# A transformer layer on one core: the stretch between the projections and the first attention head, with a store let run on, loads reordered and set-up work moved

## The reference, cut to what matters

```python
nq = _rms(x @ w_cq, g_qnorm)                      # queries through a latent of 96
q = concat([q_nope, rope(q_rope)])                # 16 heads, 32 + 64 wide
k1, v1 = ...                                      # LATENT branch: from ckv, causal
scores = (x @ w_imp)[..., 0]
_, idx = top_k(scores, KEEP); idx = sort(idx)     # KEEP = 64 tokens
sel = take_along_axis(x, idx)                     # SELECT branch
ks = (sel @ w_selk) ; vs = (sel @ w_selv)
ks = concatenate([ks[..., :NOPE], _rope(ks[..., NOPE:], cos, sin)])
kw, vw = ...                                      # WINDOW branch: from x, causal
a1 = _attn(q, k1, v1, causal=True)
a2 = _attn(q, ks, vs, causal=False)
a3 = _attn(q, kw, vw, causal=True)
out = (g[:, 0] * a1 + g[:, 1] * a2 + g[:, 2] * a3) ... @ w_proj
```

## Time and profile before

| what | us |
|---|---|
| runs, median (lowest to highest) | 2511.4 (2511.3 to 2516.3), 3 runs |
| the profiled execution, its own time | 2516.76 |
| its span in the trace | 2515.0 |
| PE busy in the span | 2213.3 (88%) |
| DVE, ACT, POOL busy | 1869.1 (74%), 1722.3 (68%), 1655.6 (66%) |
| project ends, select begins | 300.2, 310.8 |
| SP begins select's last two issues, attend begins | 377.3, 380.9 |

### The profile page before, as it was taken

One profiled execution on the slowest core, in us unless ns is written; L12 is line 12 of the kernel. 1 busy time (PEld: TensorE's weight loads), 2 busy tenths in 40 slices (PEclk: granted clock), 3 DMA queues, 4 the chain that ended last, 5 costly groups with the idle time before them and its releaser, 6 DMA issues. The chain is left out here.

```text
span 2515.0 us, 37523 instructions
## 1 busy us (share of the span) xinstructions
PE 2213.3 (88%) x11426; PEld 1863.4 (74%) x11426; DVE 1869.1 (74%) x3842; ACT 1722.3 (68%) x3574; POOL 1655.6 (66%) x1425
## 2 busy tenths in 40 slices
PE   0077678999999999999999999999999998368997
PEld 0054446888888888888888888888888886368997
DVE  2656466878888887888888788888888884356775
ACT  2433405787888878788887878888888887115775
POOL 4145506878787887878787787877777777013554
PEclk9986568999999999999999999999999999657999
DMA  9856637244444423444442434232133110624774
GB/s 380 360 186 200 237 98 213 64 93 101 95 131 98 114 77 97 95 97 134 99 114 77 98 95 96 83 68 58 31 74 71 31 18 19 153 92 136 226 211 122
DMA packets 191126, 304.34 MB, mean 121 GB/s; under 512 B 97420, under 2 KB 121484, under 8 KB 177996
## 3 DMA queue, kind: packets, MB, share of 16 engines
q1 hardware_dynamic: 181211, 289.58, 41.2%
q0 software_dynamic: 9712, 12.36, 2.4%
HBM read 206.01 MB, written 97.30 MB: 121 GB/s over the span
## 5 line engine op out<-in xcount | busy, mean ns | idle before, releaser
L1433 POOL TENSOR_TENSOR p_lo<-prob,p_hi 128x512 fp32r<-128x512 f32 (+3 forms) x1040 | 1210.6, 1180 | 372.4 <-ACT p_hi L1515 344.5
L1513 ACT ACTIVATE prob<-ps_s 128x512 f32<-128x512 f32 (+4 forms) x1344 | 727.3, 541 | 307.1 <-DVE ps_s L1759 184.0
L1515 ACT ACTIVATE p_hi<-ps_s 128x512 fp32r<-128x512 f32 (+3 forms) x1344 | 726.3, 540 | 1.6
L1651 DVE TENSOR_REDUCE max_part<-ps_x 128x1 f32<-128x512 f32 x744 | 504.4, 685 | 54.6 <-PE ps_x L1562 45.8
L1433 DVE TENSOR_TENSOR p_lo<-prob,p_hi 128x512 fp32r<-128x512 f32 (+2 forms) x240 | 214.0, 892 | 66.3 <-ACT p_hi L1515 64.3
L1649 DVE CUSTOM_DVE_ANT_0 ps_x<-ps_x,before 128x128 f32<-128x128 f32 x496 | 243.1, 492 | 25.4 <-PE ps_x L1562 19.0
L1617 PE MATMUL ps_o<-p_hi,v_lat 128*128 128x512 f32 (+3 forms) x640 | 239.4, 374 | 0.6 <-POOL p_lo L1433 0.6
L1617 PE MATMUL ps_o<-p_hi,v_win 128*128 128x512 f32 (+3 forms) x640 | 236.6, 370 | 0.0
L1619 PE MATMUL ps_o<-p_lo,v_win 128*128 128x512 f32 (+3 forms) x640 | 235.1, 367 | 0.0
L1619 PE MATMUL ps_o<-p_lo,v_lat 128*128 128x512 f32 (+3 forms) x640 | 234.6, 367 | 0.0
L1759 DVE TENSOR_TENSOR ps_s<-ps_s,mask_kq 128x128 f32<-128x128 f32 x512 | 151.7, 299 | 54.0 <-PE ps_s L1534 47.4
(11 more groups left out here) (441 smaller groups left out, 5718.9 us busy)
## 6 DMA issues: line engine op xcount, KB each, us to landing
raw<-in_experts_w_dram SPq DMA_DIRECT2D x23, 1536.0 KB
wbuf<-in_tok_weight_dram SPq DMA_DIRECT2D x16, 2000.0 KB, 16.9
head_first<-kw_scratch SPq DMA_DIRECT2D x72, 256.0 KB, 5.0
kw_scratch<-st_hi SPq DMA_DIRECT2D x48, 256.0 KB, 2.3
kw_scratch<-st_lo SPq DMA_DIRECT2D x48, 256.0 KB, 3.0
q_scratch<-st_hi SPq DMA_DIRECT2D x48, 256.0 KB, 4.6
q_scratch<-st_lo SPq DMA_DIRECT2D x48, 256.0 KB, 5.2
head_first<-q_scratch SPq DMA_DIRECT2D x48, 256.0 KB, 5.9
```

What stands on the lines that cost most here:

```text
L1433: ns.tensor_tensor(upper if low else p_lo[:, i % LSLOTS, c:CH], prob[low:P, i % NPROB, c:CH], upper.bitcast(F32), ALU.subtract).then_inc(s ...
L1513: nc.scalar.activation(prob[low:P, i % NPROB, c:CH], ps_s[i % 3][low:P, c:CH], ACT.Exp, scale=SCALE).then_inc(s["p_full"], 1)
L1515: nc.scalar.activation(p_hi[:, i % SLOTS, c:CH], ps_s[i % 3][:, c:CH], ACT.Exp, scale=SCALE).then_inc(s["p_up"], 1)
L1651: ins = nc.vector.tensor_reduce(mpart[:, q, c:c + 1], bank[:, 0:w], axis=AX.X, op=ALU.max)
```

## The change

It has four parts.

1. `g.scratch` and two semaphores `v_stored` now live through `select`. `project` no longer waits for the values' stores, and the last one (the second half of the latent branch) is issued in `select`, behind the small tables; `select` waits for both at its end. To make room, the tables and split weights that only `project` needs are freed with it.
2. `select`'s loads come in another order: queries' and window keys' high parts, then `w_selk`, `w_selv`, the tables, the values' store, then the low parts.
3. `hot` is made in 2 instructions of 8 token tiles each in place of 16, from `slots + 1` and `(position + 1) * flag`; the keys' scaling goes from DVE to ACT, the rotation and the split of the selected values from DVE to POOL; 28 row-maximum units instead of 14 stand ahead of PE's wait for the rotated keys (`beside`).
4. In `attend`, the first head's `split_up` (ACT) and `split_low` (DVE) stand at unit 3, and the gate tiles and constants (`begin`) at unit 5 of head 0, in place of ahead of unit 0.

```diff
@@ -433,13 +433,9 @@
             for t in TASKS[-2:]:
                 for o in products(t):
                     store(o)
-            if TASKS[-1][0] == "v":
-                store_values(LATENT, 1)
             sp.wait_ge(s["ust"], 16 * NJ)
             sp.wait_ge(s["tst"], 32 * NJ)
             sp.wait_ge(s["lst"], 32 * NJ)
-            for n in range(2):
-                sp.wait_ge(s[f"vst{n}"], 32)
             for n in range(NO):
                 sp.wait_ge(s[f"st{n}"], 32 * len(range(n, len(MADE), NO)))
         maxima = [(t, c) for t in range(NT) for c in range(t // 4 + 1)]
-        early, middle = 0, 14
+        early, middle, beside = 0, 14, 28
...
-            sp.dma_start(wk[:], a["w_selk"].rearrange("(k p) n -> p k n", p=P)).then_inc(s["w"], 16)
-            sp.dma_start(wv[:], a["w_selv"].rearrange("(k p) n -> p k n", p=P)).then_inc(s["w"], 16)
             for n, (half, dram, sem) in enumerate(((q_hi, g.q_dram[0], "q"), (kw_hi, g.kw_dram[0], "kw"), (q_lo, g.q_dram[1], "low"), (kw_lo, g.kw_dram[1], "low"))):
                 for r in range(3):
                     row = (0, NOPE, NOPE + HALF)[r]
                     sp.dma_start(half[row:row + NOPE, :].bitcast(F32), dram[0, r, 0:NOPE, :]).then_inc(s[sem], 16)
                 if n == 1:
+                    sp.dma_start(wk[:], a["w_selk"].rearrange("(k p) n -> p k n", p=P)).then_inc(s["w"], 16)
+                    sp.dma_start(wv[:], a["w_selv"].rearrange("(k p) n -> p k n", p=P)).then_inc(s["w"], 16)
                     sp.dma_start(ck[:], a["cos_tok"]).then_inc(s["t"], 16)
                     sp.dma_start(sk[:], a["sin_tok"]).then_inc(s["t"], 16)
+                    sp.dma_start(g.v_dram[0, :, :, 8 * DV:16 * DV].rearrange("h p n -> p h n"),
+                                 g.scratch[:, 1, :].rearrange("p (h n) -> p h n", h=H)).then_inc(g.v_stored[1], 16)
             sp.wait_ge(s["khi"], 4)
             sp.wait_ge(s["c1"], 4)
             sp.dma_start(g.ks_dram[:, 0:QA, :].rearrange("h r k -> r h k"), khi[:].bitcast(F32)).then_inc(s["st"], 16)
                              nm_t[r * NT:(r + 1) * NT, :].bitcast(F32)).then_inc(s["rows"], 16)
+            for n in range(2):
+                sp.wait_ge(g.v_stored[n], 32)
...
+            r = Count(pool, s["rot"])
+            pool.wait_ge(s["ks_read"], 3)
+            pool.wait_ge(s["t"], 32)
+            x1, x2 = ktm[:, :, NOPE:NOPE + HALF], ktm[:, :, NOPE + HALF:DQK]
+            cb = ck[:].unsqueeze(1).to_broadcast([KEEP, H, HALF])
+            sbc = sk[:].unsqueeze(1).to_broadcast([KEEP, H, HALF])
+            r.add(nc.gpsimd.tensor_tensor(kt1[:], x1, cb, ALU.mult))
+            r.add(nc.gpsimd.tensor_tensor(kt2[:], x2, sbc, ALU.mult))
+            r.add(nc.gpsimd.tensor_tensor(kt3[:], x1, sbc, ALU.mult))
+            r.add(nc.gpsimd.tensor_tensor(kt4[:], x2, cb, ALU.mult))
+            r.add(nc.gpsimd.tensor_copy(krt[:, :, 0:NOPE], ktm[:, :, 0:NOPE]))
+            r.wait()
+            r.add(nc.gpsimd.tensor_tensor(krt[:, :, NOPE:NOPE + HALF], kt1[:], kt2[:], ALU.subtract))
+            r.add(nc.gpsimd.tensor_tensor(krt[:, :, NOPE + HALF:DQK], kt3[:], kt4[:], ALU.add))
+            r.wait()
+            pool.sem_inc(s["rope"], 1)
+            pool.wait_ge(s["vone"], 2)
+            r.add(nc.gpsimd.tensor_tensor(g.v_one[:, :, 2 * DV:3 * DV], vs[:], g.v_one[:, :, DV:2 * DV].bitcast(F32), ALU.subtract))
+            r.wait()
...
             for t in range(NT):
-                pe.wait_ge(s["hot"], t + 1)
+                pe.wait_ge(s["hot"], 2 * t // NT + 1)
...
                 done = max_products(done, early + (n + 1) * (middle - early) // 4)
+            done = max_products(done, beside)
             pe.wait_ge(s["rope"], 1)
...
+            act.wait_ge(s["selr"], 1)
+            for n in range(3):
+                act.wait_ge(s["ks"], n + 1)
+                nc.scalar.activation(ktm[:].rearrange("p h d -> p (h d)")[:, n * CH:(n + 1) * CH], bank[3 + n][0:KEEP, :], ACT.Copy,
+                                     scale=sel_rstd[:, 0:1]).then_inc(s["ks_read"], 1)
             act.wait_ge(s["ks"], 4)
-            act.wait_ge(s["selr"], 1)
...
+            v.add(nc.vector.tensor_scalar(slots1[:], g.slots[:], 1.0, None, ALU.add))
             dve.wait_ge(s["pos"], 1)
-            v.add(nc.vector.tensor_copy(pos[:], bank[0][:, 0:NT]))
+            v.add(nc.vector.scalar_tensor_tensor(pos[:], bank[0][:, 0:NT], 1.0, flag[:], ALU.add, ALU.mult))
             v.wait()
-
-            for t in range(NT):
-                nc.vector.tensor_scalar(hot[:, t, :], g.slots[:], pos[:, t:t + 1], flag[:, t:t + 1], ALU.is_equal, ALU.mult).then_inc(s["hot"], 1)
+            for n in range(2):
+                c = slice(n * NT // 2, (n + 1) * NT // 2)
+                nc.vector.tensor_tensor(hot[:, c, :], slots1[:].unsqueeze(1).to_broadcast([P, NT // 2, KEEP]),
+                                        pos[:, c].unsqueeze(2).to_broadcast([P, NT // 2, KEEP]), ALU.is_equal).then_inc(s["hot"], 1)
...
-            for n in range(4):
-                if n < 3:
-                    dve.wait_ge(s["ks"], n + 1)
-                    nc.vector.tensor_scalar(ktm[:].rearrange("p h d -> p (h d)")[:, n * CH:(n + 1) * CH], bank[3 + n][0:KEEP, :], sel_rstd[:, 0:1], None,
-                                            ALU.mult).then_inc(s["ks_read"], 1)
-                done = maxima_of(done, early + (n + 1) * (middle - early) // 4)
...
-            v.add(nc.vector.tensor_tensor(kt1[:], x1, cb, ALU.mult))
-            v.add(nc.vector.tensor_tensor(kt2[:], x2, sbc, ALU.mult))
...
-            v.add(nc.vector.tensor_copy(krt[:, :, 0:NOPE], ktm[:, :, 0:NOPE]))
...
-            v.add(nc.vector.tensor_tensor(krt[:, :, NOPE:NOPE + HALF], kt1[:], kt2[:], ALU.subtract))
-            v.add(nc.vector.tensor_tensor(krt[:, :, NOPE + HALF:DQK], kt3[:], kt4[:], ALU.add))
-            v.wait()
-            dve.sem_inc(s["rope"], 1)
+            done = maxima_of(done, beside)
             half = (done + len(maxima)) // 2
...
-            dve.wait_ge(s["vone"], 2)
-            v.add(nc.vector.tensor_tensor(g.v_one[:, :, 2 * DV:3 * DV], vs[:], g.v_one[:, :, DV:2 * DV].bitcast(F32), ALU.subtract))
...
-            split_up(0, WINDOW)
             for h in range(H):
                 for i in range(NU):
+                    if h == 0 and i == 3:
+                        split_up(0, WINDOW)
...
-            for b in range(NB):
-                r = ORDER.index(b)
-                nc.vector.tensor_copy(gates[:, r, :], g.gates[:, GATE[b]:GATE[b] + 1].to_broadcast([P, NT])).then_inc(s["gset"], 1)
-            for half, b in ((k1_hi, LATENT), (kw_hi[1], WINDOW)):
-                nc.vector.tensor_copy(half[DQK:QA, :], g.onehot[DQK:QA, b:b + 1].to_broadcast([NB, T])).then_inc(s["ones"], 1)
-            dve.wait_ge(s["set"], 1)
+            def begin():
+                for half, b in ((k1_hi, LATENT), (kw_hi[1], WINDOW)):
+                    nc.vector.tensor_copy(half[DQK:QA, :], g.onehot[DQK:QA, b:b + 1].to_broadcast([NB, T])).then_inc(s["ones"], 1)
+                for b in range(NB):
+                    r = ORDER.index(b)
+                    nc.vector.tensor_copy(gates[:, r, :], g.gates[:, GATE[b]:GATE[b] + 1].to_broadcast([P, NT])).then_inc(s["gset"], 1)
+                dve.wait_ge(s["set"], 1)
             held = [()]
-            split_low(0)
...
+                    if h == 0 and i == 3:
+                        split_low(0)
+                    if h == 0 and i == 5:
+                        begin()
...
+                g.scratch = tile("scratch", [P, 2, NT * C])
+                g.v_stored = [front.enter_context(nc.semaphore(f"v_stored{n}")) for n in range(2)]
                 with ExitStack() as small:
-                    g.scratch = small.enter_context(nc.sbuf_tensor("scratch", [P, 2, NT * C], F32, side="right"))
+                    tile = lambda n, s, d=F32: small.enter_context(nc.sbuf_tensor(n, s, d))
...
```

More of the change, by code:

```diff
@@ L362, in project @@
               "ls", "lrt", "lat", "lhi", "llo", "v", "x", "x_act", "x_dve", "less", "rank", "turn", "full_act", "full_dve", "full_pool",
-              "up", "low", "st0", "st1", "st2", "ust", "tst", "lst", "vst0", "vst1", "ranks")}
+              "up", "low", "st0", "st1", "st2", "ust", "tst", "lst", "ranks")}
         block = ctx.enter_context(nc.Block())
@@ L410, in store_values @@
                 sp.dma_start(g.v_dram[1 if b == WINDOW else 0, :, :, half * 8 * DV:(half + 1) * 8 * DV].rearrange("h p n -> p h n"),
-                             values[:, half].rearrange("p h t d -> p h (t d)")).then_inc(s[f"vst{half}"], 16)
+                             values[:, half].rearrange("p h t d -> p h (t d)")).then_inc(g.v_stored[half], 16)
             row_trip(0)
@@ L603, in _ @@
                     if i == LATENT and j % 8 == 0:
-                        act.wait_ge(s[f"vst{half}"], 16)
+                        act.wait_ge(g.v_stored[half], 16)
```

(40 more changed lines are left out.)

## The result

| | before | after |
|---|---|---|
| median of the runs | 2511.4 us | 2501.46 us (2497.63 to 2503.02, 5 runs) |
| ratio, with its 95% interval | | 0.9953 [0.9938, 0.9967] |
| profiled execution, its span | 2516.76, 2515.0 | 2502.49, 2500.8 |

The kernel is faster by 0.47%, 11.8 us of 2511.4 by the ratio, which compares the runs round by round; the two medians alone differ by 9.9. 2495.8 was forecast, 15.6 less than before, with a range of 2487.5 to 2504: the measured median lies in it, 5.7 above the forecast. In us the ratio's interval is 8.3 to 15.6. The gain lies where it was expected, but is smaller.

A forecast was written before the change was run, and what follows sets the result against it. PE, busy 88% of the span, was taken to bound the kernel, so gains come only where it starves. -9.2 + 0.7 - 7.1 + 0 = -15.6 us from 2511.4 gives 2495.8 us, range 2487.5 to 2504.

The forecast's parts named there:

- Border: From project to select: without SP's wait for the values' stores, select starts 9.2 us earlier, at 301.6 (bounds 8 and 9.2).
- First product: In select: weights behind six loads land late, so their first product starts S + 16.0, 0.7 us later (S: select's start).
- the values' rest costs 1.4 us: At select's start: the first values' half still occupies the queue until S + 1.4, ahead of the six loads and weights.
- PE's readiness: Before the first weight product: shorter `hot`, gather and scales leave PE ready at S + 13.5, 1.8 us earlier than before.
- Second half: From first weight product to select's last issue: work taken off DVE's chain saves 7.1 us (bounds 4 and 9.5).
- Three `ks_tok` of 0.74: In select after the first weight product: three key copies leave DVE for ACT, counted as 1.3 us saved.
- Rotation, wait and low part: In select's later stretch: 4.2 us for rotation, about 0.9 of the transposes' wait, 0.7 for the selected values' low part.
- The clock rival: At select's weight products: weights land at S + 19, four groups may run at half clock; 8.1 us more, 2503.9; chance 0.15.
- Rotation on GpSimd: In select: 1.35 us an instruction, chain of 9.1, hidden beside the maxima with 5.6 us of slack, so costs nothing.
- if that cover were gone, all 9.1 would show: In select: without maxima beside it, the whole 9.1 us of the GpSimd chain would lengthen the kernel.
- Attend, 0: At attend's start: the sine table's load still holds PE before `prep`, so 0 gained (bounds 3.4 gained, 3 lost).

The follow-up runs named there:

- Experiment 1: Changed kernel with both values' stores issued and waited for in project again: attend's start 379.21 us against 368.61.
- experiment 4: Changed kernel with rotation and low part back on DVE behind 14 maxima: first weight product to select's last issue 52.75 us, 5.55 more.
- experiment 6: Changed kernel with attend's set-up back in one piece ahead of unit 0: `prep` 16.67 us behind attend's start against 16.52.
- experiment 7: Changed kernel with the inputs of `prep` loaded before the keys: `prep` 10.30 us behind attend's start against 16.52.
- experiment 8: Changed kernel with the inputs of `prep` loaded before the keys and attend's set-up in one piece: `prep` 13.22 us behind attend's start.
- experiment 12: The changed kernel measured once more, nothing edited: 2503.49 us, ratio to the kernel before 0.9956.
- Experiment 3: Changed kernel with weights loaded ahead of the six loads and `hot` in 16 instructions again: first weight product 15.30 us behind select's start.
- experiment 5: Changed kernel with 14 maxima instead of 28 ahead of the transposes, rotation still on GpSimd: second half 50.57 us, 3.4 longer.
- the joined kernel: Changed kernel with weights loaded first, `prep` inputs loaded before the keys, and slots counted from one without `slots_one`: 2492.29 us, ratio to before 0.9913.

## Why the prediction was off by 5.7 us

- **Border, 9.2 us: right.** 9.16 measured by S, 9.4 counted from `ranks`, which leaves out the shift of what lies ahead; the 1.4 for the border itself came out as 1.40. Experiment 1 puts the wait back.
- **First product, 0.7 later: right.** 0.73 measured, released by the weights as forecast. The bytes went through as counted, and the lag to landing was 2.0 for the 2.1 assumed, which was the middle of 1 to 3.4 and no reading: that it hit so closely is luck. That the values' rest costs 1.4 us was wrong: in experiment 1 the empty queue lost as much by its own start. PE's readiness was off too, without effect: 2.4 + 7.1 + 3.6 is 13.1, not 13.5, and it was S + 14.1, since `slots_one` took 1.9 us ahead of `hot`.
- **Second half, 7.1 us: wrong, it was 4.0.** This is the step that failed, at its lower bound of 4, and by two terms. "Three `ks_tok` of 0.74, of which I count 1.3": worth 0, since that stretch was held by PE, for which DVE waited before as well (experiment 4). And one that I had only as a rival: one more group of products on the slow clock, 3.53 us for 1.93, so 1.6. Rotation, wait and low part gave 5.55 of the 5.8 forecast. 5.6 - 1.6 = 4.0. The other kernels bear the 1.6 out: in the eleven with the rotation on GpSimd behind 28 maxima, the second half took 44.8 to 45.9 us in the five where the second group ran in 1.93, and 47.2 to 47.4 in the six where it did not. And in the changed kernel it is chance whether it comes: its own select was profiled five times (the changed kernel, experiments 6, 7, 8 and 12), slow in three and in 1.93 in two. (The term's upper bound adds to 9.7, not 9.5: 2.2 + 4.2 + 2.6 + 0.7.)
- **The clock rival: half right, and not closed.** As written, with the weights at S + 19 and all four groups slow, it did not come. It gave a pause of PE as the reason for a late rise of the clock, and I put it at 0.15. Of the 14 profiled kernels the second group of products ran slow (3.46 to 3.68 us) in seven of the nine in which PE had paused for the weights (1.65 to 2.79 us), and in one of the five in which it had not. Experiment 3 is that one: no pause, 3.52 us. Experiments 7 and 8 paused and had 1.93. So the rise falls one group earlier or later; a pause is neither needed for the late one nor enough. That the late rise is more frequent behind a pause is the count of 14 executions, too few to show it. By the Trainium skill (TensorE: Matmul & The Clock Gate, section HAM oscillation) a pause for a transfer throttles PE again; no row here shows that, since the clock was 0.50 before the pause too. Its size was as priced, 1.6 us a group (1.7 forecast), but it befell one of the three later groups, not all three.
- **Rotation on GpSimd: right.** 1.26 us each where I took 1.35, a slack of 6.6 for 5.6. What failed is "if that cover were gone, all 9.1 would show": with it gone 3.4 us showed (experiment 5), for the rest of the rotation still lay beside the first 14 maxima. The Trainium skill's advice against the move (GPSIMD Engine Reference, section 4.1) holds for the instruction, 1.26 against 0.67 us, and not for the kernel.
- **Attend, 0: right within 0.4**, and its reason is shown by experiments 6 to 8.
- **The rest of the 5.7 us.** The front gave 11.9 of the forecast's 15.6 (12.1 counted from `ranks`), so some 3.6 are accounted for, and by the ratio's 11.8 that is the whole miss. The remaining 2 are the difference between the ratio's gain and that of the two medians, 9.9. The two profiled spans differ by 14.2; 2.3 of it lie behind `prep`, where nothing was changed. From `prep` to the load of `w_proj` at mix's start the runs with that stretch unchanged took 1750 to 1754 us, but one, and from there to the end 355 to 367: that is where the runs' spread of 5 us and more comes from. So a difference of two single spans proves nothing about the front; the marks do.

## What to carry to other kernels

Cut the trace at marks that the change cannot pass, and compare from mark to mark: a term of 1.5 us shows there that drowns in the times of whole runs. Work moved off a chain saves only what that chain alone was waiting for, so ask of each moved piece what else holds that stretch (here PE held the stretch of the copies, and a transfer that of attend's set-up). When an earlier start only lengthens the next wait for a transfer, the order of the issues is the thing to change: two lines moved gave 6 to 8 us here, where the set-up spread over units gave nothing without them.

## What the runs showed of the hardware

- **DVE and GpSimd hold each other up over SBUF.** `slots_one`, 128x64, took 1.90 us beside GpSimd's cast of 1.89, and ended with it. Without it `hot` was held up. DVE's row of the joined kernel, then rows of the one that holds GpSimd back:

```profile
303.26 2.25 DVE L951 TENSOR_TENSOR hot<-slots,pos 128x512 fp32r<-128x512 f32 x2
```

```profile
303.27 1.29 DVE L952 TENSOR_TENSOR hot<-slots,pos 128x512 fp32r<-128x512 f32 x2
...
304.67 1.95 DVE L958 TENSOR_SCALAR gates<-gate_tmp 128x3 f32<-128x3 f32 x1
...
304.70 1.89 POOL L818 CAST ks_hi_all<-onehot 3x2048 fp32r<-3x2048 f32 x1 [2.28 <-DVE hot L952]
```

 With GpSimd held back `hot` takes 1.29, and the instruction that then meets the cast, three elements wide, takes 1.95 (0.33 in the changed kernel). It goes the other way too: in attend GpSimd's `p_lo` took 2.32 us beside DVE's casts of 1.22 (378.67), and 1.27 at 376.33. The Trainium skill (SBUF — State Buffer, section Who interferes with whom) says that the two share a port that one holds at a time; the rows agree.
- **An issue behind a large store can take long.** SP's row of the changed kernel, then of experiment 1, whose select has no values' store ahead of these three loads:

```profile
308.30 10.51 SPq L782 DMA_DIRECT2D head_first<-q_scratch  x3
```

```profile
317.88 1.51 SPq L786 DMA_DIRECT2D head_first<-q_scratch  x3
```

 In the twelve kernels with the store right ahead the three issues took 10.2 to 10.8 us, in the two without it 1.5. A queue without room would fit; no run shows that it is the reason. No engine waited for these loads here.
